# Feed-forward tails placed by a table of lags, a joint root in one stage, two partial sums, and a weight preparation moved into another stage

## The reference

```python
x = x + jnp.tanh(g_xattn[0]) * _L0_xattn_ref(...)
x = x + jnp.tanh(g_ffn[0]) * _L0_ffn_ref(_layernorm(x, axis=-1), ...)
x = x + jnp.tanh(g_xattn[1]) * _L1_xattn_ref(_layernorm(x, axis=-1), ...)
x = x + jnp.tanh(g_ffn[1]) * _L1_ffn_ref(_layernorm(x, axis=-1), ...)
...
```

## Time and profile before

| | before |
|---|---|
| three timed runs, us | 1315.12, 1317.58, 1316.79 |
| median, us | 1316.79 |
| profiled execution, us | 1312.83 |
| its span in the trace, us | 1311.0 |
| PE busy in the span | 1142.2 us (87%) |
| DVE / ACT / POOL busy | 58% / 52% / 28% |

### The profile page before, as it was taken

How to read it: one execution, slowest core, us unless ns; L and a number is a source line. 1 busy time by engine, 2 the same in 40 slices (tenths; PEclk the granted TensorE clock), 3 DMA queues, 4 the chain that set the end, 5 groups by cost and what they waited for, 6 DMA issues and landing times. The chain is left out here.

```text
span 1311.0 us, 24476 instructions
## 1 busy us (share of the span) xinstructions
PE 1142.2 (87%) x9697; PEld 838.0 (64%) x9697; DVE 765.1 (58%) x1671; ACT 682.4 (52%) x1205; POOL 364.4 (28%) x340
## 2 busy tenths in 40 slices
PE   1778898489999999999998599969439997999998
PEld 0567367478888888888885366643225664466667
DVE  5858535465656565656553379964537996722224
ACT  1677630165666666666654166656116665644441
POOL 3200001222222323232322422203662320744441
PEclk9999899699999999999999789989768997999999
DMA  4500000100000000000000000000000000000000
GB/s 166 189 1 1 0 1 1 65 1 1 1 1 1 1 1 1 1 2 1 1 2 1 0 2 2 2 1 0 0 0 2 2 2 2 1 0 8 9 0 17
DMA packets 6526, 16.27 MB, mean 12 GB/s; under 512 B 1312, under 2 KB 3568, under 8 KB 5520
## 3 DMA queue, kind: packets, MB, share of 16 engines
q1 hardware_dynamic: 6416, 14.74, 3.1%
HBM read 13.69 MB, written 1.05 MB: 11 GB/s over the span
## 5 line engine op out<-in xcount | busy, mean ns | idle before, releaser
L1099 POOL TENSOR_TENSOR work<-work 128x1024 f32<-128x1024 f32 x64 | 121.3, 1896 | 302.4 <-DVE work L1177 302.4
L1164 DVE TENSOR_REDUCE work<-psum 128x8 f32<-128x1024 f32 x64 | 78.0, 1219 | 93.0 <-PE psum L1000 93.0
L1116 ACT ACTIVATE work<-work 128x1024 f32<-128x1024 f32 x64 | 67.4, 1053 | 98.3 <-DVE work L1168 98.3
L1175 DVE TENSOR_REDUCE work<-work 128x8 f32<-128x1024 f32 x64 | 77.3, 1208 | 68.2 <-ACT work L1116 68.2
L1491 PEld LDWEIGHTS psum<-w_down,work 128*128 128x128 f32 x768 | 99.5, 191 | 24.4 <-issue 21.7
L887 ACT ACTIVATE work<-psum 128x512 f32<-128x512 f32 x128 | 72.8, 596 | 67.0 <-PE psum L777 66.1
L1491 PE MATMUL psum<-w_down,work 128*128 128x128 f32 x768 | 100.6, 275 | 0.7 <-DVE x L1576 0.7
L1568 DVE TENSOR_TENSOR work<-psum,big 128x512 f32<-128x512 f32 x67 | 45.8, 688 | 87.5 <-PE psum L1471 85.5
L919 DVE TENSOR_REDUCE work<-psum 128x8 f32<-128x1024 f32 x64 | 75.4, 1219 | 32.9 <-PE psum L765 18.8
L777 PEld LDWEIGHTS psum<-ident,work 128*128 128x128 f32 x512 | 57.4, 143 | 43.9 <-issue 30.7
L1168 DVE TENSOR_TENSOR work<-psum,work 128x1024 f32<-128x1024 f32 x64 | 78.4, 1225 | 6.4
(11 more groups left out here) (319 smaller groups left out, 2544.5 us busy)
## 6 DMA issues: line engine op xcount, KB each, us to landing
x<-in_x SPq DMA_DIRECT2D x1, 1024.0 KB, 4.8
ctx_tok<-in_ctx SPq DMA_DIRECT2D x1, 1024.0 KB, 6.8
ctxt<-in_ctxt SPq DMA_DIRECT2D x1, 1024.0 KB, 10.3
mask<-in_mask SPq DMA_DIRECT2D x1, 1024.0 KB, 6.5
w_down<-in_down SPq DMA_DIRECT2D x1, 1024.0 KB, 7.0
ctx_tok<-in_g SPq DMA_DIRECT2D x1, 1024.0 KB, 4.9
big<-in_u SPq DMA_DIRECT2D x1, 1024.0 KB, 6.9
out<-x SPq DMA_DIRECT2D x4, 256.0 KB, 2.2
```

Of the source, the lines that this page charges most:

```text
L1099: pool.tensor_tensor(prob[:, u % 2, h, :], prob[:, u % 2, h, :], rinv[:, u % 2, h].unsqueeze(2).broadcast_to([P, 8, P]), ALU.mult)\
L1116: act.activation(p, p, ACT.Exp).then_inc(S["exp"], 1)
L1164: dve.tensor_reduce(nmax[:, u % 2, h], s, AX.X, ALU.max, negate=True).then_inc(S["max"], 1)
L1175: dve.tensor_reduce(rsum[:, u % 2, h], prob[:, u % 2, h, :], AX.X, ALU.add).then_inc(S["sum"], 1)
```

## The change

1. `feed_forward` takes `lags`, three numbers `ROOT, NORM, TURN`, in place of the fixed 0, 1 and 3: root, normalisation and transposes are issued so many steps behind the end of a group. f0 and f1 get (1, 3, 4), f2 gets (1, 4, 5), f3 (0, 0, 0), where they are not used.
2. Means, variances and roots of all 16 blocks have a place each, so `statistics` no longer waits for the root of the group before, nor the root for the normalisation before it.
3. In f2 (`joint`) the roots of groups 0 to 2 are taken in one chain of 12 columns, at last(2)+1 = 26; their normalisations are issued at m = 29, 30, 31, and their transposes at 30, 31, 32. Group 3 keeps a root of its own (34, 37, 38).
4. In f2 a group is summed as two sums of four tiles (three additions each, six in place of seven), and both go through the down projection: eight transposed blocks instead of four. `h3` has four buffers instead of three.
5. The stage `prepare_l1` is gone. A class `Requantise` issues the same operations in f0: DVE pieces at m = 4, 7, 10 and one in every step from 11 to 22, PE pieces at m = 6, 9, 13, 19. It uses PSUM bank 3 and one 512-wide buffer instead of two.

```diff
@@ feed_forward
+    ROOT, NORM, TURN = lags
+    HALF = J // 2
+    H = 4 if one_down else 3
+    def last(g):
+        return (g + 1) * J - 1 + LAG
     def tail_at(m, late):
-        g, j = divmod(m - LAG - late, J)
-        return g if j == J - 1 and 0 <= g < NG else None
+        for g in range(NG):
+            if m == (last(NG - 2) + late + g if joint and late and g < NG - 1 else last(g) + late):
+                return g
+        return None
+    roots = [(0, NG - 1), (NG - 1, NG)] if joint else [(g, g + 1) for g in range(NG)]
@@ down, one_down
-                    pe.wait_ge(S["summed"], (g + 1) * (J - 1))
-                    h = total[:, g % 2, :]
+                    for half in range(2):
+                        pe.wait_ge(S["summed"], summed(n - HALF * (1 - half)))
+                        for b in range(GB):
+                            mm = pe.matmul(y[g % 2][:, b * P:(b + 1) * P],
+                                           total[:, g % 2, half, b * P:(b + 1) * P], tiles[j][4],
+                                           start=half == 0 and b == 0, stop=half == 1, skip_group_check=True)
@@ statistics
-                if g:
-                    dve.wait_ge(S["rstd"], g)
@@ vector
-                if not last_sub and (g := tail_at(m, 1)) is not None:
+                if not last_sub and (g := tail_at(m, NORM)) is not None:
                     normalise_group(g)
+                if q is not None:
+                    q.vector(dve, m)
@@ gpsimd
-                if not last_sub and (g := tail_at(m, 0)) is not None:
-                    reciprocal_root(g)
+                for n, (_, g1) in enumerate(roots):
+                    if not last_sub and m == last(g1 - 1) + ROOT:
+                        reciprocal_root(n)
@@ Requantise
+    def vector(self, dve, m):
+        if m == 4:
+            dve.wait_ge(k.late[1], k.late_count[1])
+            dve.memset(self.ones, 1.0)
+            for n, w in enumerate(self.weights):
+                dve.tensor_reduce(self.peak[:, n:n + 1], w[:, :], AX.X, ALU.max, apply_absolute_value=True)\
+                   .then_inc(self.peaked, 1)
...
+        elif 11 <= m <= 22:
+            n, piece = divmod(m - 11, 6)
...
+    def tensor(self, pe, m):
+        if m == 6:
...
+        elif m == 19:
+            pe.wait_ge(self.chain, 10)
@@ build
-            k.stage(prepare_l1)
```

More of the change, by code:

```diff
@@ L26 @@
 GT = GB * P
-TURN = 3
 LN_EPS = 1e-5
@@ L1391, in choose, with feed_forward @@
         dve.tensor_tensor(parts[:, :, 2, :], low, parts[:, :, 1, :], ALU.subtract).then_inc(S["parts"], 1)
-def feed_forward(k, tag, sub, tiles, function, ahead, one_down=False, routing=None, spare=(), bias=None):
+def feed_forward(k, tag, sub, tiles, function, ahead, lags, one_down=False, routing=None, spare=(), bias=None,
+                 requantise=None, joint=False):
     nc, bank = k.nc, k.bank
@@ L1486, in down @@
                     h = ring[n % R]
-                first, last = one_down or j == 0, one_down or j == J - 1
-                if first and g >= (1 if second else 2):
+                if j == 0 and g >= (1 if second else 2):
                     pe.wait_ge(S["added"], g if second else g - 1)
@@ L1491, in down @@
                     mm = pe.matmul(y[g % 2][:, b * P:(b + 1) * P], h[:, b * P:(b + 1) * P], tiles[j][4],
-                                   start=first and b == 0, stop=last, skip_group_check=True)
+                                   start=j == 0 and b == 0, stop=j == J - 1,
+                                   skip_group_check=True)
                 mm.then_inc(S["down"], 1)
@@ L1620, in accumulate, with reciprocal_root @@
                 g, j = divmod(n, J)
-                if j == 0:
+                if j % HALF == 0:
                     return
                 pool.wait_ge(S["made"], n + 1)
-                dst = total[:, g % 2, :]
-                if j == 1:
+                dst = total[:, g % 2, j // HALF, :]
+                if j % HALF == 1:
                     if g >= 2:
                         pool.wait_ge(S["down"], g - 1)
-                    before = h3[:, (n - 1) % 3, :]
+                    before = h3[:, (n - 1) % H, :]
                 else:
-                    pool.wait_ge(S["summed"], g * (J - 1) + j - 1)
+                    pool.wait_ge(S["summed"], summed(n) - 1)
                     before = dst
-                pool.tensor_tensor(dst, before, h3[:, n % 3, :], ALU.add).then_inc(S["summed"], 1)
-            def reciprocal_root(g):
-                done = [5 * g]
+                pool.tensor_tensor(dst, before, h3[:, n % H, :], ALU.add).then_inc(S["summed"], 1)
+            def reciprocal_root(n):
+                g0, g1 = roots[n]
+                done = [5 * n]
+                of = slice(g0 * GB, g1 * GB)
                 def link(ins):
@@ L1727, in _ @@
             for t in range(4):
[L1728 removed]
+                mm = pe.matmul(bank[:, t * P:(t + 1) * P], k.w["aproj"][:, t * P:(t + 1) * P],
                                k.w["bprojt"][:, :], start=True, stop=True)
[L1730 to L1735 removed]
+            mm.then_inc(self.lora, 1)
@@ L1761, in build @@
             tiles += [(cut("sup0", j), None, None, None, cut("sdown0", j)) for j in range(2)]
-            k.stage(feed_forward, "f0", 1, tiles, ACT.Silu, ahead=20, spare=(k.ctx_tok, *k.big),
+            k.stage(feed_forward, "f0", 1, tiles, ACT.Silu, ahead=20, lags=(1, 3, 4), requantise=Requantise, spare=(k.ctx_tok, *k.big),
                     routing=dict(E=16, groups=4, top_groups=2, top=4, kind="sigmoid", gate_w=w["gate0"],
@@ L1773, in build @@
                      for j in range(4)]
-            k.stage(feed_forward, "f1", 3, tiles, ACT.Gelu, ahead=2, bias=k.gated_bo[:, 3, :])
+            k.stage(feed_forward, "f1", 3, tiles, ACT.Gelu, ahead=2, lags=(1, 3, 4), bias=k.gated_bo[:, 3, :])
         if stages > 4:
@@ L1783, in build @@
                       k.sels[:, j * P:(j + 1) * P], w["comb2"][:, :]) for j in range(8)]
-            k.stage(feed_forward, "f2", 5, tiles, ACT.Silu, ahead=16, one_down=True,
+            k.stage(feed_forward, "f2", 5, tiles, ACT.Silu, ahead=16, lags=(1, 4, 5), joint=True, one_down=True,
                     spare=(k.big[0], k.big[2], k.negb),
@@ L1796, in build @@
             tiles += [(w["sg3"][:, :], None, w["su3"][:, :], None, w["sd3"][:, :])]
-            k.stage(feed_forward, "f3", 7, tiles, ACT.Silu, ahead=16,
+            k.stage(feed_forward, "f3", 7, tiles, ACT.Silu, ahead=16, lags=(0, 0, 0),
                     spare=(k.big[0], k.big[2], k.negb, k.ctxt),
```

155 lines of the change are left out of this document (82 added, 73 removed).

## The result

The changed kernel takes **1292.88 us** (median of four runs, 1291.99 to 1293.82); four runs of the kernel before, on the same chip, have a median of 1316.59 (1315.12 to 1317.58). The ratio is 0.9821 with a 95% interval of 0.9804 to 0.9838: faster, clear of the noise, by 23.7 us or 1.8%. The prediction was 1292.3, with 1287 to 1299.

The account below looks back on a forecast made before the run. PE was taken as the bound, busy 87% of the span, so edits pay only where it stands still or another engine sets the stage; 12.8 + 4.9 + 6.8 = 24.5 off 1316.79 gave 1292.3 us, range 1287 to 1299.

Parts of the forecast that it names:

- Part 1: prepare_l1 removed: 13.5 us saved, its matmuls adding 2.2 to f0's PE work, most DVE pieces free.
- the half: In f0: prepare_l1's matmuls, 4.64 us at 0.50 of the clock, take half, 2.3, at f0's full clock.
- Part 2: f0's tails with new lags: third -1.1, second -0.2 because the pieces eat the gain, first -0.2.
- Part 3: f1: transposes stand behind one more down projection, so the last addition directly follows group 2's normalisation: -4.9.
- Part 4: f2: joint root and two sums per group bring the last addition to 956.75 from 963.56: -6.8, from -11.5 to -3.5.
- every one of the twelve in turn with an addition: f2's end: all 12 normalisation instructions alternate with POOL's additions, 8.8 behind the root; f2 then about -5.4.
- The sum: Whole kernel: 12.8 + 4.9 + 6.8 = 24.5 us saved, giving 1288.3 profiled and 1292.3 against the median.
- A: f2's end: POOL and DVE block each other, root scales worse than by column; f2 -2, total 1297; chance 0.15.
- C: f0: each requantisation piece costs its own duration; parts 1 and 2 give -5, total 1300; chance 0.05.
- B: f2: power flat in columns, PE at full level in the last down; -11, total 1288; chance 0.15.
- D: Attention after f0 stays at the 1.2 GHz level about 50 us more, kernel slower than 1316.8; chance 0.02.
- E: f0 and f1: lags do nothing, root chain limits the tails; total -18, 1299; chance 0.05.

Follow-up runs that it names:

- first pair: Profiled executions of the kernel before and the changed kernel, the former the one the forecast was worked out from: 1312.83 and 1292.36 us.
- f1_old_lags: The changed kernel with f1's lags set back from (1, 3, 4) to (0, 1, 3): 1294.88 us, ratio 0.9839.
- f0_old_lags: The changed kernel with f0's lags set back from (1, 3, 4) to (0, 1, 3): 1297.77 us, a single execution.
- requant_only: The kernel before with only the requantisation moved into f0, all lags, roots and sums as before: 1306.53 us, ratio 0.9927.
- f2_root_last: The changed kernel with f2's lags (7, 8, 9) for (1, 4, 5), root and normalisations behind all additions: 1286.45 us, ratio 0.9774.
- f1_norm_behind: The changed kernel with f1's lags (1, 4, 5) in place of (1, 3, 4): 1295.82 us, ratio 0.9836.

## Why the prediction was right, point by point

**Part 1.** Holds. From f0's last addition to the attention: 21.65 before, 7.88 after, -13.8 (I had -13.5; the attention starts 0.3 behind f0's last copy, not half a microsecond). The added work on TensorE is read from the additions, counted from f0's first matmul: the first comes 0.67 later (45.28 against 44.61), the second 2.94 (65.72 against 62.78). I had 2.2 for it, less 0.2 for the first tail, with bounds 1.5 and 3.0; it is near the upper one. The wrong step is the half: the added matmuls take 0.27, 0.39, 1.12 and 1.15 in f0, 2.93 together, where half of 4.64 is 2.3. The eight of the second low-rank product, 1.15 at the full clock, took 1.91 at 0.50. Since 2.93 is all of the delay, DVE's twelve pieces ahead of m = 20 cost nothing that shows.

**Part 2.** Third tail: 13.61 before, 12.31 after, -1.3 (I had -1.1), with a select stall of 0.62, as foreseen, and transposes at 0.66 (0.8). Second tail: 14.03 before, 13.27 after, -0.8 (I had -0.2); I had the three pieces push more than they did. Both together with part 1: -12.89 against -12.8. A net cost of 2.0 that was 0.9 too small, tails that were 0.8 too small and a stage that was 0.3 more made that sum better than its parts; so far it is luck. The prediction also read all tails as one pattern, with waits of 2.0 and 1.8; f1's rows show 2.59 and 3.18, f2's 2.02 and 3.56, and its parts 3 and 4 rightly use those.

**Part 3.** Holds, mechanism and size: last addition directly behind the normalisation of group 2, -5.1 against -4.9; undoing it alone gives the same 5.1. It comes in the places foreseen: 2.1 before the third addition (I had 2.04) and 3.0 between it and the last (2.9).

**Part 4.** The additions were forecast, from the first weigh at 901.06 on, at 13.2, 23.8, 34.9 and 55.7; they came at 13.06, 23.76, 35.38 and 56.12. The root chain took 3.86 (I had 4.1), with the power at 2.30 (2.6). The normalisations beside additions cost 1.9, 0.9 and 0.9 more than their own 1.11 (I had 0.92 each), the last 16 matmuls 3.62 (3.8). The size of the contention has its price right and its count wrong: by the single instructions, each of the four additions that began beside a normalisation held one of its instructions, 1.27 to 1.30 instead of 0.33, and I had counted three. What I also had wrong is the clock: I wrote that PE is at the full one until about 936, that is 34.9 behind the first weigh, which is 923.8 here. It was not beyond 919:

```profile
900.00:912.00 12.00, 10.39 (x50) 6.11 (x48) 7.86 (x18) 4.71 (x7) 8.87 (x8) 1.00 0.00 1
912.00:919.00 7.00, 3.13 (x13) 1.03 (x12) 5.77 (x15) 0.00 (x0) 4.11 (x4) 0.90 0.00 0
919.00:945.00 26.00, 14.16 (x51) 10.07 (x51) 13.89 (x29) 1.79 (x3) 13.72 (x15) 0.50 0.00 0
```

TensorE was busy 3.1 of 7.0 us in the middle stretch. The second half of the third group's down projection, at 922.15, took 2.08, at the upper end of the 1.0 to 2.0 that I had; that fits the 0.4 by which the third addition is late, but no run tests it alone.

The rule of the Trainium skill (SBUF — State Buffer, "Who interferes with whom") on tensor_scalar and GpSimd instructions is borne out: the normalisation of four instructions that began beside two additions took 3.00, those beside one 2.04, and with nothing beside it one takes 1.08 to 1.11. What I had drawn from it as a bound, every one of the twelve in turn with an addition, isn't what came: four of the twelve were held, one for each addition. The same section says that a DVE instruction with two inputs from that memory contends as well; the piece at 210.80 is one, and POOL's four-column operation beside it took 0.57 instead of 0.23, and 0.57 or 0.58 in every kernel that has the pieces in this place. The weighs, with one input from PSUM, stayed at 0.69 beside additions.

**The sum.** -24.4 measured in the three stages of the first pair, -24.5 forecast. That the median also fits, 1292.88 against 1292.3, is partly chance. I had taken the 3.96 between the profiled execution and the median for something that stays. Part of it was a cost of the kernel before that its first trace didn't show: f0 took 3.3 more in the second trace, by the clock. The change removes the half of that which lies at the second tail, and it would have made the gain larger. In the other direction f2's routing took 4.4 more in both traces of the changed kernel, which nothing of mine contains. f3 gave 2.2 back, and the medians came out 23.7 apart.

**Rivals.** A (f2 only -2) and C (pieces at their own price) are out by the table of stretches, though A's contention is there, at 3.7 us; B's mechanism, the full clock in the last down projection, did not come: it ran at 0.50. D took no visible form: the attention of layer 1 took 444.78 and 444.88, against 445.05 and 445.03. E is refuted by f1_old_lags, where f1 alone is 5.1 longer, and by f0_old_lags.

## What stays open

f2's routing, with the same code and the same work, takes 22.11 in before, in its second profile and (22.12) in requant_only; 26.46 to 26.93 in the changed kernel and eight of its variants, and 25.06 in f1_old_lags. The rows name the means. Before:

```profile
878.95 1.07 PE L1259 MATMUL psum<-xnt,w_gate 128*32 128x512 f32 x8 [0.94 <-PEq L323]
...
885.98 13.41 PE L1456 MATMUL psum<-xnt,w_ew 128*128 128x512 f32 x28 [3.62 <-ACT big L1531]
```

After:

```profile
862.43 1.93 PE L1258 MATMUL psum<-xnt,w_gate 128*32 128x512 f32 x8 [0.94 <-PEq L322]
...
871.38 15.84 PE L1473 MATMUL psum<-xnt,w_ew 128*128 128x512 f32 x28 [3.62 <-ACT big L1558]
```

The stage starts at the 1.2 GHz level in one kernel and at the full level in the other, after the same wait of 0.94 behind the same stage. At f3 it is the other way round: the stretch of 15 us from its first matmul has a granted clock of 0.85 in before and 1.00 in after (and 0.85 in f2_root_last, which starts f3 like before). Busy time by stretch, in before:

```profile
1108.40:1123.40 15.00, 15.00 (x39) 6.23 (x40) 7.50 (x61) 10.29 (x15) 6.42 (x6) 0.85 0.00 0
```

and the same stretch in the changed kernel:

```profile
1090.10:1105.00 14.90, 14.84 (x43) 6.58 (x44) 9.50 (x67) 11.52 (x18) 8.01 (x7) 1.00 0.01 2
```

It is the same in repeated profiles of a kernel. It is not the time at which the stage starts alone: f1_norm_behind moved it by 2.9 us and left the routing at 26.83. For f3 the level goes with the version of f2, about 145 us earlier: f3 took 195.07 in every kernel with the changed f2, and 196.84 to 197.33 in every one with another f2; f2's routing was shorter only with the old f1, and in full only with the old f2 as well, so there the stage before doesn't decide alone. Nor does it for f1: in requant_only f1's first addition comes 12.71 after its first matmul, with the first three us at a granted clock of 0.50, and 11.21 in every other kernel, f0_old_lags among them, whose f0 has the same lags and pieces. No run tells what decides it. It is worth 1.5 to 4 us here and can't be had from the trace of another kernel.

## What to carry to other kernels

Place a tail step by two distances: behind the end of what it waits for (root, normalisation), and ahead of the step that waits for it, both counted in steps of the length that they have there; (1, 4, 5) moved a wait of 2.6 us from VectorE to TensorE and lost 2.9. Where two engines share a stretch that isn't bound by TensorE, let one finish its chain first, and put what only the next stage needs behind it: that was worth 6.3 us in f2, as much as all the edits of that stage together (6.1). Predict stage by stage from cuts at fixed instructions, and take a second profile before you take the difference between an execution and the median for noise.

## What the runs showed of the hardware

- Stalls of 1.4 us, twice within 3 us, or one of 1.8 behind one of 0.6, were followed by the lower clock in a stretch that was otherwise busy (transposes 1.12 instead of 0.66, eight matmuls 1.91 instead of 1.05). It came at this tail in one of two profiles of the kernel before, where the tail was 1.7 us longer behind the same stalls, and in both kernels that had the old lags beside the requantisation's pieces, where f0 was 2.3 and at least 4.2 over what I had expected. A stall of this length thus doesn't settle it.
- A power on GpSimd takes 1.04 us for 4 columns and 2.30 for 12, so by an estimate from these two 0.16 a column and 0.4 fixed; the operations of the chain around it take 0.19 to 0.25 for either.
- GpSimd and VectorE hold each other up in both directions: a normalisation of 1.11 takes 2.04 beside one addition and 3.00 beside two, one of its instructions being held for each (1.26 to 1.30 instead of 0.33), and a four-column operation on GpSimd 0.57 instead of 0.23 beside a two-input operation on VectorE.
